# A vision tower with routed experts: five-chunk routing pace, padding written after the scatter, half of each expert's down product as fp32r triples

## The reference

```
h = patches(x) @ W + b, class token, positions       # 64 images x 37 tokens, width 256
h = h + attention0(layernorm(h))                      # 16 heads, causal, relative bias
h = h + ffn0(layernorm(h))                            # below
h = h + attention1(layernorm(h))
h = h + ffn1(layernorm(h))                            # hidden 768, int8-like weights

def ffn0(x):
    expert = lambda h, g, u, d: (silu(h @ g.T) * (h @ u.T)) @ d      # hidden 704
    out = expert(x, sg, su, sd)                       # shared expert, all 2368 tokens
    probs = softmax(x @ wr.T + rb)                    # 7 routed experts
    scores, idx = top_k(probs, 2); scores /= scores.sum()
    for each token: out += scores[k] * expert_idx[k](x), k = 0, 1
```

## Time and profile before

| what | value |
|---|---|
| median of 3 runs | 1070.25 us (1068.31 to 1070.76) |
| the profiled execution: its time, its span | 1067.98 us, 1066.1 us |
| busy PE, PE weight load, DVE, ACT, POOL | 92%, 84%, 61%, 59%, 35% of the span |
| chain that ended last: PE, DVE, issue, ACT, POOL, DMA | 74%, 6%, 6%, 6%, 5%, 3% |
| 9 padding DMAs of line 334: size, median time to landing | 2064 KB (the last 1806 KB), 28 us |

### The profile page before, as it was taken

How to read it: one execution, slowest core, us unless ns; L and a number is a source line. 1 busy time by engine, 2 the same in 40 slices (tenths; PEclk the granted TensorE clock), 3 DMA queues, 4 the chain that set the end, 5 groups by cost and what they waited for, 6 DMA issues and landing times.

```text
span 1066.1 us, 28004 instructions
## 1 busy us (share of the span) xinstructions
PE 982.8 (92%) x10628; PEld 891.4 (84%) x10629; DVE 646.8 (61%) x1207; ACT 624.5 (59%) x1077; POOL 375.3 (35%) x295
## 2 busy tenths in 40 slices
PE   4987799988899996999999999999799999899998
PEld 4976688877899995999999999998678888689998
DVE  3635467775666665667667676672467776654543
ACT  3345476864556654565656656653376778655652
POOL 1343334454777770111111111112554654711210
PEclk9998899998999999999999999999899999999999
DMA  6799900005411116011111111111611100000000
GB/s 230 258 246 248 246 17 3 3 3 234 144 35 32 37 37 233 30 40 33 36 35 35 40 35 35 40 34 54 171 26 26 26 2 2 3 13 12 24 24 24
DMA packets 47517, 74.71 MB, mean 70 GB/s; under 512 B 13138, under 2 KB 38994, under 8 KB 46268
## 3 DMA queue, kind: packets, MB, share of 16 engines
q1 hardware_dynamic: 32288, 55.55, 18.7%
q0 software_dynamic: 13328, 10.66, 3.7%
q10 hardware_dynamic: 1804, 7.11, 1.7%
HBM read 41.47 MB, written 31.71 MB: 69 GB/s over the span
## 4 chain that ended last, share of the span: by engine, by line
PE 74%; DVE 6%; issue 6%; ACT 6%; POOL 5%; DMA 3%; SPq 0%; DVEq 0%; ACTq 0%; POOLq 0%
PE ps L1303 24%; PE ps L1308 14%; PE ps L1310 13%; PE ps L1309 13%; POOL routed_in L504 3%; PE ps L1708 3%; PE ps L1452 3%; PE ps L1441 2%; DMA x_in<-in_xT_dram 1%; PE ps L1691 1%; DVE Hd L1103 1%; DVE hsum L1093 1%; DMA xt<-routed_in 1%; ACT RTs L668 1%; ACT RTs L666 1%
## 5 line engine op out<-in xcount | busy, mean ns | idle before, releaser
L1206 DVE TENSOR_TENSOR tile_w<-arena,tile_w 128x1408 fp32r<-128x1408 f32 x86 | 139.5, 1622 | 77.2 <-ACT tile_w L828 77.2
L528 POOL DMA_INDIRECT routed_out<-yt,tile_to x43 | 41.2, 959 | 295.0 <-DVE yt L1228 295.0
L1308 PE MATMUL ps<-tile_w,xTs 128*128 128x352 f32 x344 | 118.8, 345 | 2.6 <-DVE xTs L1211 2.6
L1303 PE MATMUL ps<-arena,shared 128*128 x516 | 120.0, 383 | 1.0 <-ACT shared L822 1.0
L828 ACT ACTIVATE tile_w<-arena 128x1408 fp32r x86 | 118.6, 1379 | 3.3 <-issue 1.5
L1310 PE MATMUL ps<-tile_w,xTs 128*128 128x352 f32 x344 | 111.7, 325 | 0.0
L1309 PE MATMUL ps<-tile_w,xTs 128*128 128x352 f32 x344 | 111.5, 324 | 0.0
L1303 PEld LDWEIGHTS ps<-arena,shared 128*128 128x128 f32 x516 | 95.8, 192 | 12.8 <-issue 1.3
L815 ACT ACTIVATE shared<-ps 128x352 f32<-128x352 f32 x86 | 39.7, 461 | 112.6 <-PE ps L1310 112.6
L398 POOL TENSOR_TENSOR Km<-KT,cst 128x592 f32<-128x592 f32 x64 | 75.6, 1183 | 75.6 <-PE ps L1303 51.8
L969 DVE SCALAR_TENSOR_TENSOR ps<-ps,bias 128x592 f32<-128x592 f32 x64 | 50.1, 783 | 60.2 <-PE ps L1303 60.2
(11 more groups left out here) (199 smaller groups left out, 2819.0 us busy)
## 6 DMA issues: line engine op xcount, KB each, us to landing
routed_in<-zero_x SPq DMA_DIRECT2D x8, 2064.0 KB, 28.0
arena<-in_ew_dram SPq DMA_DIRECT2D x5, 2176.0 KB, 18.8
x_in<-in_xT_dram SPq DMA_DIRECT2D x7, 888.0 KB, 5.9
xt<-routed_in SPq DMA_DIRECT2D x43, 129.0 KB
arena<-in_ew_dram ACTq DMA_DIRECT2D x2, 2176.0 KB, 10.4
yg<-routed_out SPq DMA_DIRECT2D x8, 512.0 KB
out_dram<-h SPq DMA_DIRECT2D x8, 296.0 KB, 2.7
routed_in<-zero_x SPq DMA_DIRECT2D x1, 1806.0 KB, 27.8
```

Source lines behind the costliest of these rows:

```text
L1206: dve.tensor_tensor(tile_w[half][1], gate_up_of(w, half), tile_w[half][0].bitcast(F32), ALU.subtract).then_inc(s.wl, 1)
L1303: return pe.matmul(out_, lhsT, rhs, start=start, stop=stop)
L1308: pe.matmul(out_, w[1], x[0], start=start, stop=False)
```

## The change

- The padding of the whole table is gone. SP writes five single blocks of 128 rows at the end of the table at the start (POOL a sixth), and after the last group is routed, one block of 128 rows behind each expert's last row (the row numbers come from `ends`, a new copy of `place`).
- The routing of group r takes five chunks (`PACE`) instead of six, beginning at chunk 1 of group 0, so it ends with chunk 35 of 48. The normalisation of group r+1 runs along with it. `xn` and the lower part of x move from POOL to DVE (in `ffn(0)` only). The table of tiles is made in group 6.
- Tile 0 of the routed experts is loaded, transposed and split within group 7; the filler matmuls are gone. The addition of the last group (`add_y`) moves behind the first weight split on DVE.
- The loads of experts 5 and 6 move from ACT's queue to POOL's.
- The down product of each tile: three of six chunks stay plain fp32, three become `mm3`, for which ACT makes `dn_hi` and `HT_hi`, DVE `dn_lo` and `HT_lo`. The transposes lie three to a PSUM bank. `HTs` keeps the other three chunks.
- The first half of a tile's gate and up weights is split in two pieces (columns for gate, for up), each with its own semaphore count.

```diff
-            for r in range(0, ROWS, FILL * P):
-                rows = min(FILL, (ROWS - r) // P)
-                sp.dma_start(xs[r:r + rows * P, :].rearrange("(p k) d -> p k d", p=P),
-                             zero_x[:].unsqueeze(1).to_broadcast([P, rows, XW])).then_inc(s_pad, 16)
+            for k in range(1, SPARE):
+                r = EXPERTS * REGION + k * P
+                sp.dma_start(xs[r:r + P, :], zero_x[:]).then_inc(s_pad, 16)
...
+            sp.wait_ge(s_ends, 1)
+            for e in range(EXPERTS):
+                row = sp.value_load(ends[0:1, e:e + 1], min_val=0, max_val=ROWS - P)
+                sp.dma_start(xs[bass.ds(row, P), :], zero_x[:]).then_inc(s_pad, 16)
+            rows_idle(sp)
...
+        def routing_at(g, j):
+            at = len(hidden_chunks(I0)) * g + j - 1
+            return (1 + at // PACE, at % PACE) if 0 <= at < PACE * (GROUPS - 1) else (None, None)
...  POOL
+            def ffn0():
+                pool.dma_start(xs[EXPERTS * REGION:EXPERTS * REGION + P, :], zero_x[:]).then_inc(s_exl, 16)
+                for g in range(GROUPS):
+                    scatter(F[0], g, g % 2)
+                pool.wait_ge(F[0].dn_mm, LAG + 1 + 6 * GROUPS)
+                for e in range(EARLY, EXPERTS):
+                    pool.dma_start(arena[:, e * EW:(e + 1) * EW], ew[e]).then_inc(s_exl, 16)
...  ACT
+                def upper_down(t):
+                    w = weights_of(act, t)
+                    act.wait_ge(s.y_mm, t)
+                    act.activation(dn_hi, down_of(w), ACT.Copy).then_inc(s.dh, 1)
...
-                    act.activation(tile_w[half][0], gate_up_of(w, half), ACT.Copy).then_inc(s.wh, 1)
+                    for cols in pieces_of(half):
+                        act.activation(tile_w[half][0][:, cols], gate_up_of(w, half)[:, cols], ACT.Copy).then_inc(s.wh, 1)
...  DVE
+                def lower_down(t):
+                    w = weights_of(dve, t)
+                    dn_w = down_of(w)
+                    dve.wait_ge(s.dh, t + 1)
+                    dve.tensor_tensor(dn_lo01, dn_w[:, 0:2], dn_hi[:, 0:2].bitcast(F32), ALU.subtract)
+                    dve.tensor_tensor(dn_lo[2], dn_w[:, 2], dn_hi[:, 2].bitcast(F32), ALU.subtract).then_inc(s.dl, 1)
...  PE, in tile_out
-                    for j in range(6):
-                        ins = mm(ps[:, 7, 0:D], HTs[:, j], arena[:, bass.ds(w + DK * 2 * I0 + j * D, D)], j == 0, j == 5)
+                    for j in range(SPLIT, 6):
+                        mm(ps[:, 7, 0:D], HTs[:, j - SPLIT], arena[:, bass.ds(w + DK * 2 * I0 + j * D, D)], j == SPLIT, False)
+                    pe.wait_ge(s.dl, FREE + 2 * t + 2)
+                    for j in range(SPLIT):
+                        ins = mm3(ps[:, 7, 0:D], (HT_hi[:, j], HT_lo[:, j]), (dn_hi[:, j], dn_lo[j]), False, j == SPLIT - 1)
...  PE, before routed()
-                keep_going(6)
-                tile_in(0, 0, 0)
```

More of the change, by code:

```diff
@@ L1180, in step @@
                             next(first_routes[0])
-                        if l == 0 and not last:
-                            if j == 4:
-                                slots_of(g + 1, 1 - b)
-                            for _ in range((0, 1, 2, 1, 1, 0)[j] if first else (1, 1, 1, 1, 1, 0)[j]):
-                                next(routes)
-                        if l == 0 and last and j < TABLE_PIECES:
+                        if l == 0 and routing_at(g, j)[0]:
+                            routing(*routing_at(g, j))
+                        if l == 0 and g == GROUPS - 2 and j < TABLE_PIECES:
                             next(pieces)
-                        if j == MEAN_AT[l] and ahead:
+                        if l == 0 and not last and j == 3:
+                            lower_x(g + 1)
+                        if l == 1 and j == MEAN_AT and ahead:
                             dve.wait_ge(s.xn, FREE + g + 2)
                             centre(s, g + 2, 6)
-                        if l == 1 and j == VARIANCE_AT[l] - 1 and ahead:
+                        if l == 1 and j == VARIANCE_AT - 1 and ahead:
                             dve.wait_ge(s.squ, FREE + g + 3)
@@ L1196, in ffn, with add_y, tile_in @@
                 over_groups(dve, step)
-                add_y(GROUPS - 1)
+                if l == 0:
+                    tile_in(0, 0)
+                else:
+                    add_y(1, GROUPS - 1)
+            def add_y(l, g):
+                s = F[l]
+                dve.wait_ge(s.dn_mm, LAG + 1 + 6 * g + 6)
+                for m in range(DK):
+                    hm = h[:, m, group(g)]
+                    dve.tensor_tensor(hm, hm, ps[:, 4 + m, 0:N], ALU.add).then_inc(s.y, 1)
+            def tile_in(t, b):
+                dve.wait_ge(E.xh, t + 1)
+                dve.tensor_tensor(xTs[b][1], ps[:, 6, 0:D], xTs[b][0].bitcast(F32), ALU.subtract).then_inc(E.xt, 1)
@@ L1631, in step @@
                     x = lambda c: x_of(b, c)
-                    routing = l == 0 and not last
                     pe.wait_ge(s.xl, g + 1)
```

272 lines of the change are left out of this document (154 added, 118 removed).

## The result

| | before | after |
|---|---|---|
| median of the runs, us | 1069.63 (1068.31 to 1070.76, 4 runs) | 1052.89 (1050.57 to 1058.47, 4 runs) |
| profiled execution, us | 1067.98 | 1051.63 |
| its span, mean granted clock | 1066.1, 0.981 | 1049.8, 0.975 |

The ratio is 0.9856, with an interval of 0.9818 to 0.9893: the changed kernel is 1.4% faster. The forecast was 1037 with a range of 1028 to 1052. The kernel gained half of what was forecast and lies just outside the range.

The account below looks back on a forecast made before the run. PE was taken to bound the shared and routed experts, with losses in attention 0 and the seam. From 1067.98 us, -15.6 - 1 - 8 - 8 = -32.6 gave 1035.4 profiled, forecast as a 1037 median, range 1028 to 1052.

Parts of the forecast that it names:

- A: Attention 0: with the early padding fills cut, PE stops waiting for its instructions behind them, -15.6 us.
- No issue over 1 us on PE: Sign for A: in attention 0's early groups PE shows no wait named issue longer than 1 us.
- B: Shared expert: POOL's xn wait goes, DVE's xn adds small PE waits; -1 us, ends -3 and +4.
- C: Seam to the routed experts: tiles 0 to 2 start earlier, -8 us, between -9.6 and -5.5.
- H: Seam: moment when the last chunk's DVE product ends, 401.80 us before; first tile product forecast at H+5.5.
- D: Routed experts' tiles: cheaper down product saves 0.21 us a tile, if the split chain shortens too; -8 us.
- R1: Rival, chance 0.13: DVE becomes the bound of the tiles, period 7.4 to 7.5 us, total 1045 to 1051.
- R2: Rival, chance 0.09: attention 0's stalls stay, being no matter of the fills; A is 0, total 1053.
- R3: Rival, chance 0.10: at the seam rows land late or POOL's loads hold up tiles; C is -1, total 1044.

Follow-up runs that it names:

- the two padding runs: Full padding fill put back in the changed kernel: 1069.73 us, ratio 0.9955; only the new padding put in the kernel before: 1053.66 us, ratio 0.9852.
- eviction early: Changed kernel with ACT's second row eviction of each round moved from slot 4 to slot 3, ahead of the table load: 1058.2 us, ratio 0.9908.

## Why the prediction was half right

**A was right**, in size (-15.5 for -15.6) and in its signs: two groups in 39.26 us, a rate near 0 from the fourth slice (79 us) on. That it agrees to 0.1 us is luck: by the first scores of each group the second and third fell from 55.3 to 41.1 us, 2.1 over the quiet 39.0 where I had allowed 1.2, and the first, which I had not counted, gave 1.4 more. "No issue over 1 us on PE" was not: two waits are left, 2.3 us in all. That they were waits for instruction packets is still my reading, from packets and waits that stand in the same stretch; the two runs show that the fills cause them, not the way in which they do. The transfers of the packets took no longer beside the fills than after them (1.0 to 1.2 us, and 0.9 to 1.4), so if it was the packets, they waited before their transfers began, which no row shows. The Trainium skill, "Runtime: NRT & Kernel Launch" (Instruction fetch mechanics), calls the crossing of a block "mostly hidden"; that agrees with the stretch after the fills (18 packets, 3.5 us of such waits in 113 us) and, if my reading is right, not with the one beside them (7 packets, 9.6 us at one line alone in 56 us).

**B failed**, and with it the sum: -1 forecast, +10.3 measured. The step that failed is the one that says "xn(r+1) stands on DVE behind a chunk's gate and rest and ahead of PE's next logits. ACT's table reload in the chunk before leaves about no slack there, so I expect 0.2 to 0.4 us of PE wait in each of 7 rounds". The place was right, the reason too; the size was wrong. In its place the runs showed five waits for xn of up to 2.1 us (6.3 in all), 6.8 us more of idle time, and 3.6 us more in PE's matmuls at the lower clock: 1.5 us a round. Two things were missing from the working. I priced one handover, where moving the rounds from six to five chunks took the slack of every handover at once: with xn gone another was as late (160.4), and with six chunks none was, with xn on DVE all the same (149.3). And I added no clock to the waits, though the row with clock 0.88 stood in the table. Both belong to the one step: the term for the waits stood at +2 in the sum, and with the clock it measured about +13 (the 2.9 us of waits for POOL's xn and for the routing did go). The time of the table loads could have been read from the trace of before, where rsd, the second load and Silu follow each other just as in the timeline above; a chunk of PE's takes about 3.1 us, and 2.57 of loads with 1.2 of lnv, rsd and the exponential are more than that.

**C was right in its mechanism**: tile 0 at H+5.15 for H+5.5. Tile 1 came at H+12.5 for H+11.4, with PE's clock at half from 404.2 to 407.6, and the rows of tile 2 1.95 us late, inside my 0 to 2.6. In all -4.6, a little beyond the end of -5.5 that I had kept for that clock.

**D was right, and too small**: -11.4 for -8. The matmul of 256 columns is 0.117 us (0.12 forecast), so the cheaper product saves 0.24 us a tile instead of 0.21 (7.313 to 7.077, with the two pieces in both). The other 0.05 of the 0.28 comes from the period that I started from. I read one tile of 7.32 us with "nothing in it idle", but the mean of 30 is 7.359, bound by the chain over ACT and DVE, which the two pieces alone bring to 7.313. The chain mattered as the working had it: without the pieces the whole 0.28 was lost. DVE is busy 92% of the period (241.31 of 263.00), near the 95% that I worked out, and holds nothing up: rival R1 did not come. The table load of a register, 0.6 us by the Trainium skill's "DMA: Bandwidth & Descriptors" (Latency and other measured facts), can't be seen in a steady tile: no wait there has its size.

**The rest**, +1.8 at the start and +3.0 behind the tiles, I had at 0. In both, the work is nearly the same and PE's clock is lower for longer (in the 20 us from 70 us behind the last tile's transposes 0.91 instead of 1.00). From the last tile's transposes to the last scores of attention 1 it is 196.6 and 197.0 us in the kernel before and in the one with only its padding changed, and 199.6 to 203.1 in all that are built on the changed one. At the start that is scatter: in the kernels built on the changed one it is 68.3 to 71.7 us with the same work, and 71.5 in the one with only its padding changed. Behind the tiles it is not: the granted clock up to the last scores of attention 1 is 0.96 instead of 0.98. Why it falls there no experiment tried; it stays open.

By its rivals: R2 is excluded by the two padding runs. R3 had a late seam with -1; the seam was not late in the changed kernel, but it was in the one with six chunks. No rival had the shared expert in it, and that is why the range was missed: B's upper end of +4 was the only room that it had. (The sum gives 1037.7 for the median, which stands as 1037; that changes nothing.)

## What to carry to other kernels

When a rhythm is tightened, do not price the one instruction that moved: list every release that falls into the chunk that is gone, and compare it with the length of a chunk, table loads included. A profile names only the last release of a wait, so after removing it look again before counting the gain; and allow for matmuls at half clock behind PE's waits: here they came behind some of them, and added half as much again to the idle time. A step that pays only when another is made too (fewer cycles on PE, a shorter chain to it) is tested by undoing each alone.

## What the runs showed of the hardware

- Stalls of PE of 1 to 2 us can be followed by a stretch at 1.2 GHz, though not each was: of the changed kernel's stalls in the shared expert three (1.29, 2.08 and 0.94 us long) had one of 3.4 us behind them, and four of 0.9 to 1.2 us had none. With 6.8 us more of idle time went 3.6 us more in the matmuls; with "eviction early" the stage had 15.6 us idle and 156.8 us busy, 12 more than the 144.9 of nearly the same matmuls (1111 and 1109) at full clock.
- A load of 129 KB landed in 2.1 us when no other large load ran and in 10.4 us beside two loads of 2.2 MB that had been issued 5 us earlier on another engine's queue.
- A switch between Silu and the logarithm and exponential costs ACT 1.28 us each way. Leaving out the 15 of the shared expert, 19 us of ACT's time, shortened a stage that PE bounds by 17 us, since each pair held up a chunk.
